# Sums, rotations and maxima of a two-layer cross-attention kernel in smaller, evenly placed pieces, with its bulk transfers in ScalarE's queue

## The reference

```python
# per layer: x (32, 56, 256), ctx (32, 1500, 64), 16 heads
q      = rope(x_norm @ Wq' @ w_kc_q)            # 16 heads x 192
kv_r   = ctx * cos + rotate_half(ctx) * sin     # (32, 1500, 64), keys and values in one
scores = (q @ W_qr) . (kv_r @ W_kr)             # (32, 16, 56, 1500)
attn   = softmax(scores)
out    = (attn @ kv_r) @ w_kc_kv' @ Wo'
```

## Time and profile before

| | |
|---|---|
| three runs | 3784.65, 3785.76 (median), 3798.95 us |
| profiled execution | 3784.75 us, span in the trace 3783.0 us |
| busy: PE, DVE, POOL, ACT | 3122.5 (83%), 2096.5 (55%), 1654.5 (44%), 1261.1 (33%) us |
| mean granted clock of TensorE | 0.888 of full speed |
| attention of layer 0, rows 0 to 5, 4 passes | 882.1 us |
| attention of layer 1, rows 0 to 5, 4 passes | 715.5 us |

### The profile page before, as it was taken

The page is one execution under the profiler, slowest core; times in us unless marked ns, Lnnn a source line. Parts: engine busy times, 40 slices in busy tenths (PEclk is TensorE's granted clock), DMA queues, the critical chain, the costliest instruction groups (busy, mean ns, idle before and its releaser), DMA issues. The chain is left out here.

```text
span 3783.0 us, 43017 instructions
## 1 busy us (share of the span) xinstructions
PE 3122.5 (83%) x16008; PEld 1727.9 (46%) x16008; DVE 2096.5 (55%) x2343; ACT 1261.1 (33%) x1747; POOL 1654.5 (44%) x952
## 2 busy tenths in 40 slices
PE   7678988788887789887888768986998789877997
PEld 6434446444474344553444534453444444454445
DVE  3566656666466665666665545454554455445545
ACT  3123333133341334332333323422343234322442
POOL 0445534555435455244653235611662156414651
PEclk9789989898988899888999879987998899888998
DMA  6323203132112322132220232113221312122310
GB/s 230 113 53 79 53 33 102 45 79 57 47 55 76 76 64 46 53 92 57 64 68 31 71 89 70 35 44 78 67 51 46 78 47 69 49 49 52 80 56 10
DMA packets 117803, 247.48 MB, mean 65 GB/s; under 512 B 30416, under 2 KB 82880, under 8 KB 110039
## 3 DMA queue, kind: packets, MB, share of 16 engines
q1 hardware_dynamic: 117590, 244.57, 24.5%
HBM read 171.24 MB, written 48.27 MB: 58 GB/s over the span
## 5 line engine op out<-in xcount | busy, mean ns | idle before, releaser
L1317 DVE TENSOR_REDUCE maxpart<-pair 112x2 f32<-112x1000 f32 x768 | 920.4, 1198 | 739.8 <-PE pair L840 739.8
L1204 POOL TENSOR_TENSOR sums<-sums,prob 125x896 f32<-125x896 f32 x472 | 1016.5, 2154 | 305.1 <-ACT prob L1091 259.5
L1091 ACT ACTIVATE prob<-wide 125x896 f32<-125x896 f32 x768 | 704.3, 917 | 941.1 <-PE wide L866 931.6
L881 PE MATMUL single<-prob,kv 125*64 125x448 f32 x3072 | 772.4, 582 | 0.9
L840 PE MATMUL pair<-kparts,qhigh 64*112 64x500 f32 x1536 | 403.4, 522 | 286.5 <-DVE maxpart L1317 264.1
L840 PEld LDWEIGHTS pair<-kparts,qhigh 64*112 64x112 f32 x1536 | 143.3, 183 | 820.7 <-DVE maxpart L1317 595.9
L861 PE MATMUL wide<-qhigh,kparts 64*125 64x448 f32 x3072 | 491.0, 399 | 0.0
L1204 POOL TENSOR_TENSOR sums<-prob 125x896 f32<-125x896 f32 x64 | 133.8, 2091 | 623.8 <-ACT prob L1091 623.8
L861 PEld LDWEIGHTS wide<-qhigh,kparts 64*125 64x125 f32 x3072 | 278.4, 193 | 160.2 <-issue 130.4
L866 PE MATMUL wide<-shift,ones_row 64*125 64x448 f32 x1536 | 296.7, 382 | 44.0 <-DMA shift<-maxrow 44.0
L861 PE MATMUL wide<-qlow,kparts 64*125 64x448 f32 x1536 | 295.5, 380 | 0.0
(11 more groups left out here) (314 smaller groups left out, 4250.0 us busy)
## 6 DMA issues: line engine op xcount, KB each, us to landing
kparts<-keys_merged SPq DMA_DIRECT2D x64, 750.0 KB, 9.1
wexp_low_values<-in_experts SPq DMA_DIRECT2D x68, 384.0 KB, 3.1
kparts<-kparts SPq DMA_DIRECT2D x96, 250.0 KB, 3.1
keys_merged<-kparts SPq DMA_DIRECT2D x32, 750.0 KB, 8.6
recip<-zrec_merged SPq DMA_DIRECT2D x112, 112.0 KB, 2.8
raw<-in_ctx SPq DMA_DIRECT2D x33, 375.0 KB
w_low_values<-w_merged SPq DMA_DIRECT2D x64, 192.0 KB, 2.4
values_merged<-kv SPq DMA_DIRECT2D x32, 375.0 KB
```

Of the source, the lines that this page charges most:

```text
L881: mm = pe.matmul(mix_acc[64 * half:64 * half + DC, 0:HQ], kv[:, j % 3, t, :], prob[:, (j * LT + t) % NPROB, half * HQ:(half + 1) * HQ], st ...
L1091: nc.scalar.activation(prob[:, n_ % NPROB, :].rearrange("p (a b) -> p a b", a=2), acc[0:LP, :, 0:HQ], ACT.Exp)\
L1204: nc.gpsimd.tensor_tensor(dst, first_in, prob[:, n_ % NPROB, :], ALU.add).then_inc(s["pool_sum"], 1)
L1317: V.tensor_reduce(maxpart[:, j % 2, t:NMAX:4, b], acc[0:TQ, :, 0:LB], AX.X, ALU.max).then_inc(*R.signal_drained(kind, *key))
```

## The change

- `POOL_TILES` goes from 10 to 11. POOL makes 10 additions in a row instead of 9; on DVE the two additions become one, of `prob` 11 and POOL's sum.
- Layer 0's `rope` is split into halves of 384 elements: cosine halves at t = 1 and 2 (`ropecos`), additions at t = 3 and 4. Before, all of it stood at t = 3.
- `smax` stands behind `norm`, `maxT` and `keyT` of its tile instead of ahead of them. `spread` moves from t = 3 to t = 8, `share` from t = 11 to t = 10.
- The stores (`stash`, now at t = 9), the loads of `raw` (at the third `keyT`) and layer 1's `fetch` (t = 2 instead of 1) are issued by ACT, in its own queue.
- In the prologue the maxima of row 0 come one in a step; the last ones and row 1's first three use the two `wide` regions beside `pair`; only the fourth piece of row 1 stands behind `maxneg`. Row 1's `rotate`, `rope` and `keyT` move from the end of layer 0's prologue to heads 6 to 11. The three `keyT` of row 0 use three regions.

```diff
-POOL_TILES, POOL_LAST = 10, 5
+POOL_TILES, POOL_LAST = 11, 5
...
+    def rope(j, parts=(0, 1)):
+        for part in parts:
+            add("ropecos", j, part)
+        for part in parts:
+            add("rope", j, part)
...
-            if n >= 7 and n % 4 == 3 and n < H:
-                for c in range(3):
-                    add("smax", 0, n // 4 - 1, c, region=PAIR)
+            if n >= 6 and (n - 6) % 4 < 3:
+                add("smax", 0, (n - 6) // 4, (n - 6) % 4, region=PAIR)
+            if n == 6:
+                add("stash", 0)
+                add("rotate", 1)
+            if n == 7:
+                rope(1)
...
+        for i in range(3):
+            maximum(1, i, (0, 1, PAIR)[i])
+        add("query", NPAIR - 1, region=2)
+        for c in range(3):
+            add("smax", 0, 3, c, region=(0, 1, PAIR)[c])
...
-            if layer == 1 and t == 1 and 2 < j + 2 < BG:
+            if layer == 1 and t == 2 and 2 < j + 2 < BG:
                 add("fetch", j + 2)
...
-            if ahead[0] < BG:
-                maximum(*ahead)
             last = (j, t)
             if t == 1 and j:
                 add("norm", j - 1, region=3)
+            if j + 1 < BG and t == 9:
+                add("maxT", j + 1, region=3)
             if layer == 0 and t in (5, 6, 7) and j + 2 < BG:
                 keys(j + 2, t - 5)
-            if t == 3 and j:
+            if layer == 0 and t == 9 and j + 2 < BG:
+                add("stash", j + 2)
+            if ahead[0] < BG:
+                maximum(*ahead)
+            if t == 8 and j:
                 add("spread", j - 1)
-            if t == SHARE_AT[2] and j:
+            if t == 10 and j:
                 add("share", j - 1, 2)
...
-            if layer == 0 and t == 3 and j + 2 < BG:
-                add("rope", j + 2)
+            if layer == 0 and t in (1, 2) and j + 2 < BG:
+                add("ropecos", j + 2, t - 1)
+            if layer == 0 and t in (3, 4) and j + 2 < BG:
+                add("rope", j + 2, t - 3)
...
+                    if kind == "stash":
+                        j, = key
+
+                        act.wait_ge(s["rope_done"], 2 * (j + 1))
+                        act.dma_start(scratch["values"][BG * g + j], kv[:, j % 3, :, :].rearrange("p t d -> p (t d)"))\
+                            .then_inc(s[f"values_moved_{j % 3}"], 16)
+                        for b in range(3):
+                            act.wait_ge(*R.drained("keyT", j, b))
+                        act.dma_start(scratch["keys"][BG * g + j], kparts[0:DC, j % 3, :, :].rearrange("p a l -> p (a l)").bitcast(F32))\
+                            .then_inc(s[f"keys_moved_{j % 3}"], 16)
...
-                        dve.wait_ge(s["dve_sum"], vector_sums(j + 1) - 1)
+                        other = sum_dve
+                        if vector_sums(j + 1) - vector_sums(j) == 1:
+                            dve.wait_ge(*R.drained("score", j, LT - 1))
+                            if j:
+                                dve.wait_ge(*R.filled("norm", j - 1))
+                            other = prob[:, (j * LT + LT - 1) % NPROB, :]
+                        else:
+                            dve.wait_ge(s["dve_sum"], vector_sums(j + 1) - 1)
                         dve.wait_ge(s["pool_sum"], pool_sums(j) + pool_tiles(j) - 1)
-                        V.tensor_tensor(sum_dve, sum_dve, sum_pool[:, j % 2, :], ALU.add).then_inc(s["dve_sum"], 1)
+                        V.tensor_tensor(sum_dve, other, sum_pool[:, j % 2, :], ALU.add).then_inc(s["dve_sum"], 1)
```

More of the change, by code:

```diff
@@ L36 @@
 ZP, ZC = 56, 8
-SHARE_AT = (1, 9, 11)
 RT = NT // 112
@@ L87, in schedule @@
     if layer == 0:
-        add("rope", 0)
+        rope(0)
         for c in range(3):
-            keys(0, c)
-        for n in range(H + 2):
-            if n == H - 3:
-                add("rotate", 1)
-            if n == H:
-                add("rope", 1)
+            add("keyT", 0, c, region=3 + c)
+        for n in range(H + 1):
             if n + SPLIT_AHEAD < H:
@@ L101, in schedule @@
                 add("query", (n - 3) // 2, region=2)
-            if n >= 7 and n % 4 == 3 and n < H:
-                for c in range(3):
-                    add("smax", 0, n // 4 - 1, c, region=PAIR)
+            if n >= 6 and (n - 6) % 4 < 3:
[5 more added lines that the diff above has]
+                rope(1)
+            if 9 <= n < 12:
+                keys(1, n - 9)
+            if n == 12:
+                add("stash", 1)
+        for i in range(3):
[3 more added lines that the diff above has]
+            add("smax", 0, 3, c, region=(0, 1, PAIR)[c])
     else:
@@ L111, in schedule @@
             add("query", p, region=p % 3)
-            if p >= 3 and p % 2:
-                for c in range(3):
-                    add("smax", 0, p // 2 - 1, c, region=PAIR)
-    last_maxima(0)
+            if p >= 4:
+                add("smax", 0, (p - 4) // 3, (p - 4) % 3, region=PAIR)
+        for n in range(4, 9):
+            add("smax", 0, n // 3, n % 3, region=(PAIR, 0, 1)[n % 3])
+        for c in range(3):
+            add("smax", 0, 3, c, region=(PAIR, 0, 1)[c])
+        for i in range(3):
+            maximum(1, i, (PAIR, 0, 1)[i])
     add("maxneg", 0)
-    if layer == 0:
-        keys(1, 0)
+    maximum(1, 3)
     add("maxT", 0, region=3)
-    if layer == 0:
-        keys(1, 1)
-        keys(1, 2)
-    for n in range(EARLY_MAX):
-        maximum(1, n)
     last = None
```

68 lines of the change are left out of this document (29 added, 39 removed).

## The result

| | before | after |
|---|---|---|
| median | 3785.95 us | 3617.24 us (3614.29 to 3622.73) |
| ratio, 95% interval | | 0.9549 [0.9525, 0.9572] |
| profiled execution, its span | 3784.75, 3783.0 us | 3614.29, 3612.5 us |
| mean granted clock | 0.888 | 0.904 |
| attention of layer 0, rows 0 to 5 | 882.1 us | 851.7 us |

The change is 4.5% faster. The forecast was 3453 us, 8.8% faster, and its range (3375 to 3560) does not hold the time. "Between the attentions" is from the last exponential of a pass to the first of the next; it holds the prologue and the work around it that did not change. Rows 6 and 7 and the tail moved by 1.3 us or less each.

A forecast was written before the change was run, and what follows sets the result against it. PE was taken as the floor of the attention rows. Gains of 144 and 60 us in the attentions of layers 0 and 1, and 80 and 48 in their prologues, sum to 332: 3784.75 to 3453 us, range 3375 to 3560.

The forecast's parts named there:

- PE is the floor: Attention middle rows: PE's busy time bounds them, 27.3 us in layer 1 and 29.6 us in layer 0.
- `shift`, `recip` and `stash` together: Layer 0's row end: the 44.0 us wait for `shift` goes; 0.5 us a row added, bounds 0 and 4.
- A small DMA in another queue passes between the packets.: DMA queues: a small DMA passes a large one in another queue, so the 44.0 us `shift` wait goes.
- Rival 2: Own queue does not help small DMAs: `shift` keeps 44 us, `recip` costs 56; 3553 us, chance 0.16.
- +1.5: Layer 1's prologue: row 0's keys share wires with head weights, +1.5 us a pass; total -48, bounds -64 and -24.
- Layer 1's attention: Layer 1, rows 0 to 5: DVE loses a sum and the `packed` wait; 655 against 715.5 us, -60.
- `rope` in pieces: Layer 0's rows: halves of `rope` mostly fit DVE's free time; 0.3 us lost a row, bounds 0 and 5.6.
- part (b): Layer 0's prologue behind head 15: 19 of 31 us remain to the first exponential, -12 us.
- Part (c): Layer 0's prologue: three-region `keyT`, head weights not waiting behind the first store; -4.5 us, bounds 0 and 11.
- ACT's issues at 0: Layer 1's rows: three `fetch` issues on ACT, below 1.8 us, cost nothing; `stash` likewise.
- Rival 3: Bulk issues hold ACT during handover, some 12 us in 24 rows and 17 in 20; 4080 us, chance 0.04.
- Rival 1: Layer 0's PE clock stays at 0.91, losing 3.4 us a row; 3535 us, chance 0.14.

The follow-up runs named there:

- x6: x3 with `spread` moved from t = 8 to t = 4 in layer 0 and t = 7 in layer 1: 3391.27 us, 0.8953.
- x1: The changed kernel with `stash` moved from t = 9 of its row to t = 3 of the next row: 3508.10 us, 0.9242.
- x11: The kernel before with only layer 0's stores of keys and values issued by ACT, at t = 9: 3774.08 us, 0.9956.
- x12: The kernel before with stores (t = 9), `raw` (third `keyT`) and `fetch` (t = 1) all in ACT's queue: 3802.58 us, 1.0025.
- x3: The changed kernel with `fetch`, `stash` and `raw` issued by SP again, at the same steps: 3428.14 us, 0.9029.
- x4: The changed kernel with layer 1's fetches of rows 0 to 2 issued by SP behind the eight head weights: 3572.64 us, 0.9418.
- x2: The changed kernel with `spread` back at t = 3: 3676.92 us, 0.9687.
- x13: x6 with `POOL_TILES` back at 10, so DVE does both sums again: 3393.21 us, 0.8945.
- x10: x3 with all four pieces of layer 0's `rope` at t = 3: 3544.85 us, 0.9356.
- x8: The changed kernel with keys stored and fetched in three DMAs of 2,000-byte rows for each one of 12,000-byte rows: 3643.79 us, 0.9616.

## Why the prediction was right and wrong

- **PE is the floor.** Right, but the floor was put too high: PE's 27.3 us of a row of layer 1 held 0.8 us that the same matmuls do not need. x6 runs that row in 26.5 us. In layer 0 it is busy for 28.3 us where the floor was put at 29.6.
- **`shift`, `recip` and `stash` together, "I add 0.5 us", "bounds 0 and 4".** This is the step that failed. The changed row of layer 0 is 5.1 us above the 31.0 of the forecast. Its 36.1 us are 28.3 of matmuls (x6), 2.5 more of them at the lower clock, 3.7 of waiting for `shift` where 0.5 was allowed, 1.2 for the rotation, and 0.4 of other idle time. x1 gives 103 us back, 4.3 a row, by moving `stash` alone. The chain was read link by link rightly (reciprocal, store, `recip`, `share`), but each link was given the duration that it has with no bulk beside it: 1.5 us for a store that took 3.4 behind a doubling slowed by `raw`, and 2.8 for a `recip` that took 5 to 6 beside `stash`. The end of 4 us was also no true bound, since a doubled chain was not put in for both waits.
- **"A small DMA in another queue passes between the packets."** Wrong here. In x11 `shift` has its queue to itself, and PE waits 43.5 us for it against 44.0 and goes on when the store lands, give or take some 1 us. The rule on queues that the prediction weighed (the Trainium skill, Trainium Kernel Development and Optimization, Key Constraints) had nothing to be won for `shift`, and x11 and x12 agree with it. The trace goes further than that rule, by which several issuing engines only save issue time: with the changed steps the second queue lost about 190 us. The Trainium skill (DMA: Bandwidth & Descriptors, Queues, rings and completion order) says that a DMA's completion on each DMA engine is signalled only after that engine's earlier writes, across its queues. The 3.5 KB store agrees with it: it lands 0.2 us after the doubling ahead of it, be it in 3.4 us (the changed kernel) or 3.6 (x3). But no run here parts this from a plain sharing of the wires.
- **Rival 2** named the right mechanism at 3553 us. It kept `shift` at 44 us where it rose to 101, and gave `recip` 2.8 us in 20 rows of the 56 that wait, and it had no price for the head weights. That is how the time came to lie above it.
- **Layer 1's prologue, "+1.5" for shared wires.** Wrong in size. x4 takes the sharing away, with some of ACT's issues, and gives 48.6 us back, 12.2 a pass. The bound of -24 in all was on the wrong side of the measured -8; the row that spoke against it was in the forecast's own argument for layer 0, where head weights behind one store made ACT wait up to 10.7 us.
- **Layer 1's attention** came in at -59 for -60, but not wholly for the reasons given. The wait for `packed` is gone, which needed `spread` late (x2). The sum, which the forecast counted as a gain, is worth nothing by x13. `share` beside POOL's sum, priced at 0.25 us on PE, cost more: in front of the row from 2628.4 DVE's `ctx_n` takes 2.09 us instead of 0.6, and PE is idle for 1.1. The PE floor was 0.8 us a row lower than thought, and that hid the error: 26.5 + 1.1 is 27.6. That the total came in is luck; x6 gets -78.
- **`rope` in pieces.** Right in the main. In a middle row of the changed kernel the four took 0.55, 1.08, 1.33 and 1.33 us, within the 0.5 to 1.5 forecast. The loss was put at 0.3 us and in the wrong place: PE waits 1.2 us a row for the last piece at the first transposes, and 1.1 still in x6's row. x10 prices the opposite at 5.0 us a row; 2.7 of them are waiting, the rest is the clock, so that it comes near the far bound of 5.6 by chance. The rule on the port (the Trainium skill, SBUF — State Buffer, SBUF: two separate sides) agrees as before: pieces of 0.55 us where POOL is idle, up to 2.4 where it runs back to back.
- **Layer 0's prologue.** Right in its total, -74 for -80, and in part (b): 19.8 us from head 15's rotation to the first exponential in the second pass for a forecast of 19. Part (c) did not come as told: ACT's wait for head weights rose from 44.2 to 60.9 us, the longest from 10.7 to 11.1.
- **ACT's issues at 0.** Right for the two or three in a row of this kernel: behind its three issues in the row from 2628.4 PE is not idle. x8 shows the limit: seven cost PE 2.9 us. Rival 3's mechanism, that an engine stands still while a transfer is handed over, did not come for ACT in these rows, but it did for SP, 3.1 us at the second `recip`, and for ACT in x8's prologue.
- **The clock.** The forecast let it rise to 1.00 in layer 0 with the stalls gone. In the changed kernel the stalls stayed, and it was 0.93 there; in x3 and x6, with fewer, it was 0.99. So it followed the idle time. Rival 1, by which it stays low in a dense PE, falls, but each stall was paid twice: in the row of 36.1 us the same matmuls took 2.5 us more than in x6's of 29.8.

Together: of 332 us forecast, 168.7 came. The second queue took about 190, and `spread` at t = 8 behind the load of `raw` another 30 in the two attentions (x3 to x6); with neither, x6 lies 62 us below the forecast, since PE's floor was lower than assumed. What stays open is how much of the small DMAs' lateness is the length of the bulk's packets and how much its sheer volume; x8 shows that the first matters for `shift` and for layer 1's head weights, and hardly for `recip`.

## What to carry to other kernels

Issue a small DMA that an engine waits for when no bulk is under way, or ahead of it in the same queue; in this kernel a second queue took that order away and gave nothing for it. Price every DMA of a chain by rows where bulk runs beside it, and ask for each moved transfer what small ones go out in the same few microseconds. Take a gain from a shorter piece of work only where the row shows somebody waiting for it: one sum less on DVE was worth nothing, one rotation spread over four tiles about 120 us. And price a stall with the clock that it costs: here 43 of 112 us.

## What the runs showed of the hardware

- A DMA of 3.5 KB landed in 1.4 us with nothing ahead of it. Issued 3.0 us behind one of 250 KB in its own queue, with a load of 375 KB under way, it landed 0.2 us after that one, in 2.9 to 3.7 us, whether the load stood in the same queue (x3) or in another (the changed kernel, x1).
- Two DMAs of 1.8 KB issued 1.3 to 2.4 us behind a 750 KB store released PE 0.4 us after the store's landing from the same queue, and in the median 0.2 us after it from another (x11). The waits over 24 rows were 44.0, 43.5 and 44.2 us.
- An engine can be held in the issue itself: SP's second issue of `recip` took 3.1 us beside the stores and 0.6 without. ACT's issues took 0.3 to 0.7 us each in the rows shown, six took 8.4 us in one prologue of x8, and they hold back its own work.
- The granted clock followed PE's idle time in layer 0's attention: 0.93 with 127 us idle in four passes (the changed kernel), 0.99 with 58 (x3) and with 36 (x6). It was not 1.00 in every dense row: row 0 of layer 1, without idle time, had 0.97.
